# Adding a residual by accumulating DMAs of GpSimd instead of a VectorE operation, in a two-network graph kernel

## What is computed

```
h = max(layernorm(x), 0)
x = x + elu(softmax(mask(leaky_relu(f1_i + f2_j))) @ h)         # first network, one attention layer
h = max(layernorm(x), 0)
for l in 0..2:                                                   # second network
    a = softmax(mask(leaky_relu(si_i + sj_j + b_l))) @ h
    u = layernorm(h + a) * g1[l] + beta1[l]
    h = layernorm(u + gelu(u @ W1[l] + b1[l]) @ W2[l] + b2[l]) * g2[l] + beta2[l]
x = x + h
```

## Time and profile before

| | |
|---|---|
| median of 3 runs | 2825.91 us (2825.34 to 2826.56) |
| profiled execution, its time | 2823.76 us |
| its span, first to last instruction | 2821.6 us |
| TensorE matmuls busy | 2676.8 us, 95% |
| VectorE busy | 2328.0 us, 83% |
| ScalarE busy | 2145.9 us, 76% |
| GpSimd busy | 1594.2 us, 56% |
| DMA | 201.34 MB, mean 71 GB/s |
| mean granted TensorE clock | 0.98 |

### The profile page before, as it was taken

One profiled execution on the slowest core, in us unless ns is written; L12 is line 12 of the kernel. 1 busy time (PEld: TensorE's weight loads), 2 busy tenths in 40 slices (PEclk: granted clock), 3 DMA queues, 4 the chain that ended last, 5 costly groups with the idle time before them and its releaser, 6 DMA issues.

```text
span 2821.6 us, 53323 instructions
## 1 busy us (share of the span) xinstructions
PE 2676.8 (95%) x16773; PEld 2399.6 (85%) x16868; DVE 2328.0 (83%) x8541; ACT 2145.9 (76%) x3978; POOL 1594.2 (56%) x2051
## 2 busy tenths in 40 slices
PE   3588999999999999999999999999999999999997
PEld 2477888988898988989888889898888889989987
DVE  7877888888888898888888888889888877777774
ACT  5476887877778787878777878778787776776774
POOL 5335555566666555555666555555666554554564
PEclk8699999999999999999999999999999999999999
DMA  6211212122222112122322121211222121111111
GB/s 204 88 40 57 68 65 79 44 79 79 98 79 78 61 62 79 65 75 66 98 70 84 65 75 64 71 61 63 87 91 87 59 61 38 48 51 45 56 62 53
DMA packets 118015, 201.34 MB, mean 71 GB/s; under 512 B 12737, under 2 KB 85473, under 8 KB 117729
## 3 DMA queue, kind: packets, MB, share of 16 engines
q1 hardware_dynamic: 117728, 197.87, 21.6%
HBM read 113.95 MB, written 83.89 MB: 70 GB/s over the span
## 4 chain that ended last, share of the span: by engine, by line
PE 69%; DVE 15%; POOL 6%; issue 5%; ACT 4%; DMA 0%; DVEq 0%; POOLq 0%; SPq 0%; ACTq 0%; another core or an unknown queue 0%
PE bank L564 32%; PE bank L549 26%; PE ps_u L523 5%; DVE g_lo L893 3%; DVE st L867 3%; POOL xo L351 3%; PE ps_u L606 2%; PE ps_s L518 2%; POOL hb L351 2%; POOL rs L1153 2%; DVE ub L974 1%; DVE ub L946 1%; PE ps_s L510 1%; DVE vb L862 1%; ACT g_hi L775 1%
## 5 line engine op out<-in xcount | busy, mean ns | idle before, releaser
L564 PE MATMUL bank<-w_hi,g_hi 128*128 128x256 f32 x3072 | 891.5, 290 | 14.9 <-DVE g_lo L893 14.4
L775 ACT ACTIVATE g_hi<-bank,b_eff 128x512 fp32r<-128x512 f32 x768 | 529.1, 689 | 456.0 <-PE bank L549 451.2
L564 PE MATMUL bank<-w_hi,g_lo 128*128 128x256 f32 x3072 | 865.2, 282 | 0.0
L564 PE MATMUL bank<-w_lo,g_hi 128*128 128x256 f32 x3072 | 864.2, 281 | 0.0
L549 PE MATMUL bank<-zt_hi,w_hi 128*128 128x512 f32 x1536 | 647.8, 422 | 23.3 <-DVE vb L1081 9.5
L893 DVE TENSOR_TENSOR g_lo<-bank,g_hi 128x512 fp32r<-128x512 f32 x768 | 516.9, 686 | 183.2 <-ACT bank L777 170.5
L549 PE MATMUL bank<-zt_hi,w_lo 128*128 128x512 f32 x1536 | 608.9, 396 | 0.0
L549 PE MATMUL bank<-zt_lo,w_hi 128*128 128x512 f32 x1536 | 607.3, 395 | 0.0
L564 PEld LDWEIGHTS bank<-w_hi,g_hi 128*128 128x128 f32 x3072 | 578.9, 188 | 25.5 <-DVE g_lo L893 24.3
L564 PEld LDWEIGHTS bank<-w_lo,g_hi 128*128 128x128 f32 x3072 | 579.3, 189 | 0.8
L564 PEld LDWEIGHTS bank<-w_hi,g_lo 128*128 128x128 f32 x3072 | 578.7, 188 | 0.0
(11 more groups left out here) (86 smaller groups left out, 4193.2 us busy)
## 6 DMA issues: line engine op xcount, KB each, us to landing
xb<-x_scratch SPq DMA_DIRECT2D x88, 512.0 KB, 4.0
x_scratch<-xo SPq DMA_DIRECT2D x64, 512.0 KB, 4.9
xin<-in_x SPq DMA_DIRECT2D x40, 512.0 KB, 4.6
r_scratch<-elu_r SPq DMA_DIRECT2D x32, 512.0 KB, 3.0
xin<-r_scratch SPq DMA_DIRECT2D x32, 512.0 KB, 4.8
out<-xo SPq DMA_DIRECT2D x32, 512.0 KB, 3.5
m<-m_scratch SPq DMA_DIRECT2D x96, 128.0 KB, 3.5
x_scratch<-h SPq DMA_DIRECT2D x24, 512.0 KB, 2.9
```

Source lines behind the costliest of these rows:

```text
L564: mm = pe.matmul(y, g[:, c, r * P:(r + 1) * P], w[:, l, c, :], start=(c == 0 and n == 0), stop=(c == C - 1 and n == 2))
L775: act.activation(g_hi[:, c, :], block_in, ACT.Gelu, bias=bias).then_inc(g_hi_ready, 1)
```

## The change

`elu_sums` ends with elu_sum: the third operation, L1035, is gone, and xin[1] is no longer loaded with x. At the end of its step's own work and ahead of `affine`, GpSimd waits for elu_sum and issues four DMAs, one for each graph (128 rows of 1 KB), each of which reads x from HBM and adds it to elu_r in SBUF. Their semaphore, x1_in, counts 16 for each DMA. SyncE and VectorE wait for all 64 of it where they waited for x1_ready; GpSimd waits for neither before `affine`. The -1 isn't added to the elu any more: r_scratch and the norm's input are then greater by one in every element. The norm takes a constant shift out again, and for the last residual beta2 of the last layer is lowered by one, by one small VectorE operation in the set-up.

```diff
-                if v2 is not None and v2 < CH:
-                    if v2:
-                        sp.wait_ge(x1_ready, st.nth0(v2 - 1))
-                    sp.dma_start(xin[1][:, :, :], pick(x_u, st, v2)).then_inc(xr_in, 16)
...
                 if v3 is not None and v3 < CH:
-                    sp.wait_ge(x1_ready, st.nth0(v3))
+                    sp.wait_ge(x1_in, 16 * T * st.nth0(v3))
                     sp.dma_start(pick(r_u, st, v3), elu_r[:, :, :]).then_inc(r_out, 16)
...
                 if v2 is not None and v2 >= CH:
-                    sp.wait_ge(x1_ready, st.nth0(v2))
+                    sp.wait_ge(x1_in, 16 * T * st.nth0(v2))
...
+                link(dve.tensor_scalar(beta2_row[:, L - 1, :], beta2_row[:, L - 1, :], -1.0, None, ALU.add))
...
-                        dve.wait_ge(x1_ready, st.nth0(v3))
+                        dve.wait_ge(x1_in, 16 * T * st.nth0(v3))
                         statistics(elu_r, st3, st3_ready)
...
                         ins.then_inc(elu_sum, 1)
-                        dve.wait_ge(elu_sum, st.nth0(v2))
-                        if v2 < CH:
-                            dve.wait_ge(xr_in, 16 * st.nth0(v2))
-                        dve.scalar_tensor_tensor(out=elu_r.rearrange("p t d -> p (t d)"),
-                                                 in0=elu_r.rearrange("p t d -> p (t d)"), scalar=-1.0,
-                                                 in1=residual_x(v2).rearrange("p t d -> p (t d)"),
-                                                 op0=ALU.add, op1=ALU.add).then_inc(x1_ready, 1)
...
+                def residual_sum():
+                    if v2 is not None:
+                        pool.wait_ge(elu_sum, st.nth0(v2))
+                        rows = pick(x_u, st, v2)
+                        for t in range(T):
+                            pool.dma_start(elu_r[:, t, :], rows[:, t, :], accum_op=ALU.add).then_inc(x1_in, 16)
+
...
                 mask()
                 first_mask()
+                residual_sum()
 
                 if live(s - 1) and s - 1 < U - 1:
...
-                    if v2 is not None:
-                        pool.wait_ge(x1_ready, st.nth0(v2))
                     affine(pool, st, s - 1)
                     residual(pool, st, s - 1)
```

More of the change, by code:

```diff
@@ L208, in build @@
         xin_in = sem("xin_in")
-        xr_in = sem("xr_in")
         r_out = sem("r_out")
@@ L265, in build @@
         elu_sum = sem("elu_sum")
-        x1_ready = sem("x1_ready")
+        x1_in = sem("x1_in")
         st3_ready = sem("st3_ready")
@@ L312, in only_middle @@
             return middle(s) is not None and early(s) is None and late(s) is None
-        def residual_x(v):
-            return xin[1] if v < CH else xin[0]
         def made(v):
```

## The result

The changed kernel takes **2893.28 us** (median of 4 runs, 2891.38 to 2895.77) against 2825.62 of before (4 runs beside it): ratio 1.024, 95% interval 1.0222 to 1.0258. It is 67.7 us slower than before, and outside the range of the forecast (2818 to 2851). The profiled execution has a span of 2890.5 us.

The account below looks back on a forecast made before the run. TensorE was taken to bound most steps, VectorE the step after `late` work, with the start a pipeline being filled. +6.6 in six steps and -1.8 at the start gave +4.8 on 2825.91, about 2831 us; range 2818 to 2851.

Parts of the forecast that it names:

- Four make 4.1 us (bounds 1.4 and 6.2): GpSimd's hold by the four DMA issues, at 1.02 us each, the median of its power on 128x4.
- the six steps: Steps 19, 22, 43, 46, 67, 70, where GpSimd also adds the last residual: 1.1 us lost in each, +6.6 us.
- Cost 0 in 18 of the 24 steps: Ordinary steps of groups 8 to 31: the affine comes 2.8 us later, the inverse root's reader is not delayed.
- 4.6 us of slack: Room on GpSimd between affine and L974, the inverse root's reader, in the 18 ordinary steps.
- from 5.9 on all 24 pay: From a GpSimd hold of 5.9 us on, every one of the 24 steps of groups 8 to 31 loses time.
- 1.7 to spare: Room before L974 in the steps where GpSimd also adds the last residual; a delay of 2.8 leaves 1.1 us.
- Gain: 0 in each of the 24 steps: Removing L1035 in groups 8 to 31: VectorE would only wait 1.2 us longer, gaining nothing.
- Landing, 3.5 us: Time for a 128 KB accumulating transfer to land, taken from the load of m; upper bound 7.0.
- rival 3: Accumulate lands late, 7.0 us: xin 1.5 us too late in 23 steps, about 2875 us; chance 0.05.
- The start, -1.8: Groups 0 to 7: later xin[0] costs groups 0 and 1, L1035's removal gains afterwards; net -1.8 us.
- Rival 2: GpSimd held long, 1.5 us an issue, 6.0 in all: sum +21.8, 2848 us; chance 0.24.
- Rival 1: Cheap issue, 0.35 us per DMA, 1.4 in all: steady part 0, start gains, 2819 us; chance 0.18.

Follow-up runs that it names:

- hold_8: Changed kernel without its DMAs (first network's residual left out), eight small powers on GpSimd in their place for groups 8 to 31: 2827.31 us.
- ring_1216: Changed kernel with dynamic_dma_scratch_size 1216 instead of 1024, nothing else edited: 2826.41 us, ratio 1.0005.
- hold_3: As hold_8, but with three small powers on GpSimd instead of eight: 2812.77 us, ratio 0.9959.
- ring_2368: Changed kernel with dynamic_dma_scratch_size 2368 instead of 1024, nothing else edited: 2825.87 us, ratio 1.0002.
- early_1216: Changed kernel with 1216 bytes, DMAs only for groups 0 to 7 (issued before the low halves, xin[0] loaded earlier), VectorE's operation from group 8: 2820.21 us.
- ring_2560: Changed kernel with dynamic_dma_scratch_size 2560 instead of 1024, nothing else edited: 2848.66 us, ratio 1.0078.
- plain_copy: Changed kernel with its four DMAs as plain copies without the addition, so x overwrites the elu: 2819.35 us (one run).
- orders_1216: ring_1216 with the DMAs ahead of the weights' low halves in steps -5 to -3 and SyncE's xin[0] load ahead of its x1_in wait: 2829.06 us.

## Why the prediction was wrong

- **"Four make 4.1 us (bounds 1.4 and 6.2)"** is the step that failed. Its form was wrong, not only its size: it priced an issue as an instruction with a duration, from a power's row, and no row of before could show that an issue may wait for the landing of earlier transfers. Nor did a row show that hardly any of a power on 128x4 is data: one on 128x1 takes 0.54 us (hold_8) against 1.02. Measured, an issue that does not wait is 0.54 to 0.68 us behind the one before (once 0.81), and four of them put the next operation 2.7 to 3.2 us after the elu's end (in ring_1216); one that waits is 3.2 to 5.2 us behind. So the affine came at 5.4 to 9.3 instead of 4.1.
- **The forecast for the issue that doesn't wait**: 1.02 us was too dear, 0.35 too cheap. ring_1216, the kernel that the forecast described, has start -2.3 (forecast -1.8) and the six steps +8.2 (forecast +6.6); its median is 2826.4, beside the forecast 2831, within the band of no change of before. That the +8.2 lies so near +6.6 is in part luck: the hold is shorter than the 4.1 forecast (2.7 to 3.2), and the 1.35 us by which the affine's first four operations are longer, which the forecast did not have, make up for it.
- **"Cost 0 in 18 of the 24 steps"** rested on 4.6 us of slack. The slack is right (hold_8), but at a hold of up to 9 us it is used up: +31.9. The prediction had said that from 5.9 on all 24 pay.
- **"1.7 to spare" in the six steps**: right, shown by hold_8 and hold_3. Only the delay put against it was wrong: +33.4 instead of +6.6.
- **"Gain: 0 in each of the 24 steps" for L1035**: right. The step is 28.40 as before, and the wait ahead of L1081 (now L1065) went from 1.15 to 2.40. That ahead of g_lo remained at 2.12, since it hangs on the new step's matmuls.
- **Landing, 3.5 us**: right for the changed kernel (median 3.3). In the rings that never stall, where four are under way together, it is 4.1; the longest of them all took 6.2 us (ring_2368), under the upper bound of 7.0 that rival 3 takes; the waiters behind x1_in still lose nothing in the steady part. In the changed kernel VectorE never waits for xin in it, as forecast (in ring_2368 once, 0.2 us).
- **The start, -1.8**: +11.0 measured. In the changed kernel its groups have gaps at numbers 3, 6, 7, 9, 14 and so on. For the same steps ring_1216 gives -2.3, near the -1.8, as the working would have it without the gaps; but start columns differ by up to 3 us between kernels alike there, so this doesn't prove each of its terms.
- **The rivals.** Rival 2 (GpSimd held long) has the right path: affine, root, L974, the six steps first and then all. Its cause, a dearer issue, and its size (6.0 us held, 2848) were not right. The gaps go by the DMA's number, and vanish with a ring of 1216 or 2368 bytes beside the same VectorE work. Rival 1's price of an issue (0.35) was too low, rival 3 did not come.
- **Not foreseen:** in all 13 kernels the steps behind step 5 outside the 24 are 2 to 7 us shorter in sum, 2.4 to 4.1 of it in step 48 alone, which was 31.1 us long before. It is also there in early_1216, where VectorE's operation still stands in that step, so the operation's going is not its cause. Step 48 is the first of the loop's second round, and VectorE stands ahead of L1081 in it for 5.1 us before and 2.6 to 3.0 us in the others, with no releaser that the profile shows. What it is I have not settled.

## What to carry to other kernels

An issue of a DMA on GpSimd had no fixed price here, 0.54 to 0.81 us behind the one before or 3.2 to 5.2: look in the trace whether some issues of a burst stand still, count them from the start of the program, and see whether their numbers are multiples of a period that `dynamic_dma_scratch_size` moves. Then lay a delay on GpSimd against the slack of its reader, and count it to the end of the work between, not to its start. Here a burst of four wanted a ring that holds four or eight of them, and 192 more in `dynamic_dma_scratch_size` gave back 67 us. Before that, put the work whose reader is near ahead of the issues on GpSimd, and the issues behind it; that was worth another 9.6 us.

## What the runs showed of the hardware

- Where GpSimd stands still between two issues of a burst (ahead of the multiples of 3 and of 7 with 1024 in `dynamic_dma_scratch_size`, of 9 and of 17 with 2560), it goes on once the DMA ahead has landed: 0.20 to 0.40 us after it in the 41 gaps of the changed kernel, 0.20 to 0.27 in the 17 of ring_2560, 0.40 in the 14 of plain_copy. Start to start that is 3.2 to 5.2 us in the changed kernel, where a DMA lands in 3.3 (median), and 2.6 to 3.3 in plain_copy, where it lands in 2.4.
- With 1024 the accumulating DMAs of 128 rows, counted from the start of the program, have their gaps at every 3rd and every 7th (the changed kernel), plain copies at every 7th alone (plain_copy). With 1216 and 2368 none of the 96 issues behind the first of a group stands still.
- Right behind four accumulating DMAs GpSimd's next four operations are slower, 4.20 us instead of 2.83 (ring_1216); behind four plain copies they are not (2.80, plain_copy).
- An operation of VectorE took longer beside some of GpSimd's: the dot on L854 7.05 us instead of 0.41 beside the low halves (orders_1216), and the small one on L869 1.07 instead of 0.17 beside the affine (the changed kernel).
